# Mixture-of-experts overflow rows in units of 32, in four column groups of TensorE

## The reference

```python
def xattn(query, key):
    a = einsum('bqd,bkd->bqk', query, key)
    return einsum('bqk,bkd->bqd', softmax(a), key)

def ffn(x, W_gate, b_gate, W_e, b_e):
    logits = x @ W_gate + b_gate
    _, top_idx = top_k(logits, 2)
    y_all = relu(einsum('bsd,edh->bseh', x, W_e) + b_e)
    return take_along_axis(y_all, top_idx[..., None], axis=2).mean(axis=2)

x = x + tanh(g_xattn[0]) * xattn(layernorm(x), ctx_4096)
x = x + tanh(g_ffn[0]) * ffn(layernorm(x), W_gate, b_gate, W_e, b_e)
```

## Time and profile before

| | us |
|---|---|
| median of 3 runs | 349.36 |
| lowest, highest | 346.36, 354.34 |
| profiled execution, its own time | 346.13 |
| its span, first to last instruction | 344.2 |

### The profile page before, as it was taken

The page is one execution under the profiler, slowest core; times in us unless marked ns, Lnnn a source line. Parts: engine busy times, 40 slices in busy tenths (PEclk is TensorE's granted clock), DMA queues, the critical chain, the costliest instruction groups (busy, mean ns, idle before and its releaser), DMA issues.

```text
span 344.2 us, 4282 instructions
## 1 busy us (share of the span) xinstructions
PE 316.2 (92%) x1488; PEld 231.1 (67%) x1488; DVE 203.3 (59%) x434; ACT 123.0 (36%) x165; POOL 77.7 (23%) x97
## 2 busy tenths in 40 slices
PE   0989999989999999969999999999999999999960
PEld 0554465555565588748887788888888888888840
DVE  2226368477668886895566885755176675753220
ACT  2223444346435548012544535515031551431000
POOL 6101131110213210402422331530121233111130
PEclk9999999999999999999999999999999999999996
DMA  7999999999989895218999999898469889644142
GB/s 257 309 270 333 348 352 398 392 315 385 375 302 353 303 391 170 70 54 207 398 312 397 368 354 330 237 383 258 63 178 350 269 219 390 189 61 63 18 76 30
DMA packets 24333, 90.57 MB, mean 263 GB/s; under 512 B 2898, under 2 KB 2898, under 8 KB 24302
## 3 DMA queue, kind: packets, MB, share of 16 engines
q1 hardware_dynamic: 13662, 52.86, 42.4%
q0 software_dynamic: 7504, 25.47, 27.6%
q10 hardware_dynamic: 3136, 11.83, 9.9%
HBM read 73.63 MB, written 16.52 MB: 262 GB/s over the span
## 4 chain that ended last, share of the span: by engine, by line
PE 72%; DMA 15%; DVE 6%; issue 2%; ACT 2%; POOL 1%; SPq 0%; DVEq 0%; POOLq 0%
PE ps L442 47%; PE ps L350 9%; PE ps L375 8%; DMA kT<-in_ctx_cols 7%; DMA raw<-in_L_ffn_W_e 4%; PE ps L425 4%; DVE wl L871 3%; DMA xg<-hn_rows,src_token 3%; PE ps L396 2%; PE ps L387 1%; DMA x_all<-in_x 1%; PE ps L341 1%; DVE xl L875 1%; ACT qT L601 1%; DVE stats L728 1%
## 5 line engine op out<-in xcount | busy, mean ns | idle before, releaser
L871 DVE TENSOR_TENSOR wl<-raw,wh 128x1024 fp32r<-128x1024 f32 x64 | 75.7, 1219 | 18.7 <-ACT wh L622 18.6
L442 PE MATMUL ps<-wh,xh 128*128 128x512 f32 x256 | 83.1, 401 | 1.7 <-DVE xl L875 1.7
L442 PE MATMUL ps<-wl,xh 128*128 128x512 f32 x256 | 80.7, 394 | 1.9 <-DVE wl L871 1.9
L442 PE MATMUL ps<-wh,xl 128*128 128x512 f32 x256 | 80.2, 393 | 0.0
L622 ACT ACTIVATE wh<-raw 128x1024 fp32r<-128x1024 f32 x64 | 64.0, 1052 | 29.9 <-DMA raw<-in_L_ffn_W_e 23.0
L442 PEld LDWEIGHTS ps<-wl,xh 128*128 128x128 f32 x256 | 47.8, 188 | 13.4 <-DVE wl L871 2.8
L442 PEld LDWEIGHTS ps<-wh,xl 128*128 128x128 f32 x256 | 48.0, 188 | 10.6
L1054 POOL DMA_INDIRECT out_rows<-y,dst_token x15 | 29.7, 1978 | 109.7 <-DVE y L885 100.3
L442 PEld LDWEIGHTS ps<-wh,xh 128*128 128x128 f32 x256 | 46.3, 189 | 11.3 <-DVE xl L875 2.6
L625 ACT ACTIVATE xh<-ps 128x1024 fp32r<-128x1024 f32 x16 | 16.3, 1020 | 88.8 <-PE ps L425 88.8
L350 PE MATMUL ps<-kT,qT 128*100 128x361 f32 x128 | 44.0, 496 | 1.6 <-ACT qT L601 1.3
(11 more groups left out here) (122 smaller groups left out, 237.5 us busy)
## 6 DMA issues: line engine op xcount, KB each, us to landing
raw<-in_L_ffn_W_e SPq DMA_DIRECT2D x64, 512.0 KB, 9.9
kT<-in_ctx_cols SPq DMA_DIRECT2D x16, 722.0 KB, 16.8
ctx<-in_ctx ACTq DMA_DIRECT2D x8, 1024.0 KB, 13.1
bias<-in_L_ffn_b_e SPq DMA_DIRECT2D x8, 512.0 KB, 12.5
ctx<-in_ctx ACTq DMA_DIRECT2D x8, 420.0 KB, 16.3
out_rows<-x_all POOLq DMA_DIRECT2D x8, 400.0 KB
hn_rows<-hn POOLq DMA_DIRECT2D x8, 400.0 KB
x_all<-in_x SPq DMA_DIRECT2D x7, 400.0 KB
```

The lines of the kernel that those rows point to most:

```text
L442: mm = nc.tensor.matmul(into[:, n * HB:(n + 1) * HB], rows[:, k, :], weights[:, k, n * HB:(n + 1) * HB], start=(k == 0 and c == first), st ...
L871: nc.vector.tensor_tensor(wl[e % 2][:, k, :], raw[e % 2][:, k, :], wh[e % 2][:, k, :], ALU.subtract).then_inc(s_wl, 1)
```

## The change

Rows over the static tiles go in units of 32 rows instead of tiles of 128, up to OVER = 17 units for an expert, so that COLS becomes 8 x 25 = 200. A unit's rows are gathered (32 rows), turned by eight transposes with a 32 x 32 identity, and copied from PSUM by ACT as plain float32 (`x_over`, 128 x 256); neither ACT nor DVE splits them. The product is float32: for each slice k and for each of `wh` and `wl`, four matmuls of 256 columns, the c-th with the c-th quarter of the weights' columns, into PSUM partitions 32c to 32c+31. DVE adds the bias in four instructions on 32 partitions each, and POOL adds 128 quarter rows to the output. The number of units is worked out by the same rule as before, with 32 in the place of 128. In `name_tokens` the static tiles' slots are read in four copies, a quarter of the partitions each, and the units' slots are kept apart and named once, by the new `name_overs`, called between the splits of expert 1's weights, just before `fill_table`.

```diff
+    UNIT = 32
+    GROUPS = P // UNIT
+    HQ = H // GROUPS
+    OVER = -(-HALVES * (HALF_TOK - P) // UNIT)
+    UNITS_E = STATIC_TILES * GROUPS + OVER
+    COLS = E * UNITS_E
...
-        over_rows = sb("over_rows", [P, D])
-        xh_over = sb("xh_over", [P, KD, P], F32R)
-        xl_over = sb("xl_over", [P, KD, P], F32R)
+        over_rows = sb("over_rows", [UNIT, D])
+        x_over = sb("x_over", [P, KD, UNIT])
+        over_y = sb("over_y", [P, HQ])
...
             def turn_over(over_before, j):
-                pe.wait_ge(o_gath, 16 * (over_before + j) + 16)
-                turn_rows(ps[1], over_rows).then_inc(o_xT, 1)
+                wait_apart(pe, o_gath, 16 * (over_before + j) + 16)
+                for k in range(KD):
+                    mm = nc.tensor.transpose(ps[1][:, k * UNIT:(k + 1) * UNIT], over_rows[:, k * P:(k + 1) * P],
+                                             ident[0:UNIT, 0:UNIT])
+                mm.then_inc(o_xT, 1)
...
                 for k in range(KD):
-                    mm = multiply(xh_over, xl_over, e % 2, k, over_ps, (HH, HL, LH), HH, LH)
+                    for w in (wh[e % 2], wl[e % 2]):
+                        for c in range(GROUPS):
+                            mm = nc.tensor.matmul(over_ps[c * UNIT:(c + 1) * UNIT, :], x_over[:, k, :],
+                                                  w[:, k, c * HQ:(c + 1) * HQ].bitcast(F32),
+                                                  start=(k == 0 and w is wh[e % 2]), stop=(k == KD - 1 and w is wl[e % 2]))
...
             def name_tokens(half):
                 dve.wait_ge(s_slots, HALF_B * (half + 1))
-                if half == 0:
-                    link(nc.vector.tensor_copy(acc[:, :], slot_ps))
-                else:
-                    link(nc.vector.tensor_tensor(acc[:, :], acc[:, :], slot_ps, ALU.add))
+                units = slot_ps.rearrange("p (e u) -> p e u", e=E)
+                first = half * (UNITS_E - GROUPS)
+                for c in range(GROUPS):
+                    rows = slice(c * UNIT, (c + 1) * UNIT)
+                    last = nc.vector.tensor_copy(slot_acc[rows, :], units[rows, :, first + c])
+                link(last)
...
+                units = units[:, :, GROUPS:GROUPS + OVER]
                 if half == 0:
+                    nc.vector.tensor_copy(over_acc[:, :, :], units).then_inc(s_over_read, 1)
                 else:
+                    dve.wait_ge(s_over_read, 1)
+                    link(nc.vector.tensor_tensor(over_acc[:, :, :], over_acc[:, :, :], units, ALU.add))
+
+            def name_overs():
+                link(nc.vector.tensor_scalar(over_used[:, :, :], over_acc[:, :, :], 0.0, own_shift[:, 0:1], ALU.is_lt,
                                              ALU.mult))
+                link(nc.vector.scalar_tensor_tensor(out=src_over[:, :, :], in0=over_acc[:, :, :], scalar=own_row[:, 0:1],
+                                                    in1=over_used[:, :, :], op0=ALU.add, op1=ALU.add))
+                link(nc.vector.tensor_scalar(over_used[:, :, :], over_acc[:, :, :], 0.0, spare_shift[0][:, 0:1], ALU.is_lt,
+                                             ALU.mult))
+                link(nc.vector.scalar_tensor_tensor(out=over_used[:, :, :], in0=over_acc[:, :, :],
+                                                    scalar=spare_row[0][:, 0:1], in1=over_used[:, :, :],
+                                                    op0=ALU.add, op1=ALU.add))
+                link(nc.vector.tensor_scalar(dst_over[:, :, :], over_used[:, :, :], float(GROUPS), quarter_no[:, 0:1],
+                                             ALU.mult, ALU.add))
...
                 if k == KD // 2:
+                    name_overs()
                     fill_table()
...
-                    add_rows(over_rows, idx_over[:, 1:2], o_added)
+                    quarters = out.rearrange("n (a d) -> (n a) d", a=GROUPS)
+                    g.indirect_dma_start(quarters, bass.IndirectOffsetOnAxis(idx_over[:, 1:2], 0), over_y[:, :], None,
+                                         compute_op=ALU.add).then_inc(o_added, 16)
```

More of the change, by code:

```diff
@@ L638, in wait_multiplied, with copy_over @@
                     eng.wait_ge(s_wfree, KD * (e + 1))
-            def split_over(over_before, j):
+            def copy_over(over_before, j):
                 act.wait_ge(o_xT, over_before + j + 1)
-                split_rows(xh_over, ps[1]).then_inc(o_xh, 1)
+                nc.scalar.activation(x_over[:, :, :].rearrange("p k m -> p (k m)"), ps[1][:, 0:KD * UNIT], ACT.Copy
+                                     ).then_inc(o_x, 1)
             def load_values(b):
@@ new lines, in name_tokens @@
+                link(nc.vector.scalar_tensor_tensor(out=src_token[:, half, :], in0=slot_acc[:, :], scalar=own_row[:, 0:1],
+                                                    in1=is_used[:, :], op0=ALU.add, op1=ALU.add))
+                link(nc.vector.tensor_scalar(is_used[:, :], slot_acc[:, :], 0.0, spare_shift[half][:, 0:1], ALU.is_lt,
+                                             ALU.mult))
+                nc.vector.scalar_tensor_tensor(out=dst_token[:, half, :], in0=slot_acc[:, :],
+                                               scalar=spare_row[half][:, 0:1], in1=is_used[:, :], op0=ALU.add, op1=ALU.add
+                                               ).then_inc(s_tokens, 1)
@@ L844, in name_tokens @@
[L844 to L847, removed]
-                                             ALU.mult))
@@ L852, in count_first_half @@
             def count_first_half():
                 dve.wait_ge(s_count, 1)
-                link(nc.vector.tensor_scalar(skip[:, :], count_ps, float(P), float(-TILES_E * P), ALU.max, ALU.add))
+                link(nc.vector.tensor_scalar(skip[:, :], count_ps, float(P), float(-UNITS_E * UNIT), ALU.max, ALU.add))
             def fill_table():
@@ L905, in evacuate_over @@
                 dve.wait_ge(o_mm, n + 1)
-                finish(over_ps, e, over_rows, o_yev, n + 2, o_y)
+                for c in range(GROUPS):
+                    rows = slice(c * UNIT, (c + 1) * UNIT)
+                    last = nc.vector.tensor_tensor(over_y[rows, :], over_ps[rows, :],
+                                                   bias[e % 2][rows, c * HQ:(c + 1) * HQ], ALU.add)
+                last.then_inc(o_yev, 1)
+                dve.wait_ge(o_yev, n + 2)
+                nc.vector.tensor_scalar(over_y[:, :], over_y[:, :], 0.0, tgf_half[:, 0:1], ALU.max, ALU.mult
+                                        ).then_inc(o_y, 1)
             norm(0, measure_query(0), 1, 2)
             dve.wait_ge(s_const, 1)
+            link(nc.vector.tensor_scalar(quarter_i[:, :], row_i[:, :], 5, None, ALU.logical_shift_right))
+            link(nc.vector.tensor_copy(quarter_no[:, :], quarter_i[:, :]))
             norm(1, measure_query(1), 1, 2)
@@ L1048, in gather_tile @@
                     pool.wait_ge(s_xT, n - 1)
-                col = column(*ORDER[n])
-                half = ORDER[n][1]
-                gather(xg[n % 2], src_token[:, col:col + 1], s_gath[n % 2], hn_rows[0:HALF_TOK * (half + 1), :])
+                e, half = ORDER[n]
+                gather(xg[n % 2], src_token[:, half, e:e + 1], s_gath[n % 2], hn_rows[0:HALF_TOK * (half + 1), :])
             def add_rows(rows, idx, added):
@@ L1132, in _ @@
             gather_tile(3)
[L1133 removed]
             for part in range(2):
[L1135 removed]
+                g.tensor_scalar(half_row[:, part:part + 1], dst_token[:, HALVES - 1, E - 1:E], 2.0, float(part), ALU.mult, ALU.add
                                 ).then_inc(s_half_row, 1)
```

77 lines of the change are left out of this document (34 added, 43 removed).

## The result

| | before | after |
|---|---|---|
| median | 349.05 us (4 runs) | 367.63 us (4 runs, 365.84 to 370.11) |
| ratio | | 1.0557, 95% interval 1.0497 to 1.0617 |
| profiled execution, its span | 344.2 us | 368.4 us |

What follows compares the result with a forecast made beforehand. PE was taken to bound the kernel, with DVE's naming at 139 to 153 us also on the chain. -4.0 - 0.3 + 0.4 + 0.4 + 1.75 gave about -1.75 us, put on the median 349.36: 347.6 us, range 343.5 to 355.0.

Steps and rivals of the forecast that it cites:

- How many units: Over path: expert 4 has 18 rows over 128, one unit of 32; all others none, so it is taken once.
- The product, -4.0 us: PE's over-tile product: 64 float32 matmuls, four quarters at once, take 7.1 us where it was 11.14.
- Rival 1: PE's unit product: the four quarters run one after another, 27.5 us, kernel 368.0 us; chance 0.16 including fewer than 1.7 at once.
- Rival 2: PE's unit product: quarters run at once but weight loads don't hide, 10.3 us, kernel 350.9; chance 0.14 shared with two at once.
- The 8.7 us: PE's unit product by the Trainium skill's column-group share, 3.2 times for four; whole sum 1.6 us higher.
- rival 4: Over path: several units for expert 4, each another 7 us or more; within the remaining chance of 0.02.
- The turn, -0.3: PE's eight transposes of the unit's rows, within tile 8's products: 0.6 us in place of 0.88.
- The slots, +0.4: PE's slots products: tok_col goes from 56 to 200 columns, 0.065 us more, twice per batch; bounds 0 and 1.1.
- `name_overs`, +1.75: DVE amid expert 1's splits, ahead of fill_table: five linked steps on 136 elements, 1.75 us; bounds 1.3 and 2.2.
- `name_tokens(1)`, +0.4: DVE's naming from the last slots to the first split: 1.75 us where it was 1.39; bounds 0.1 and 0.8.
- The delay at full price: DVE's time added before tile 2 moves the whole stretch behind it and reaches the end in full.
- Rival 3: Stretch behind 153 us set by DMA: DVE's added 2.55 us vanish, only -4.3 is left, kernel 345.1 us; chance 0.06.

Runs made afterwards that it cites:

- e1: Changed kernel without PE's code for an expert's second and further units, which never runs here: 349.39 us, ratio to before 0.9943.
- e5: Kernel before, with the never-run product of an expert's second over tile written five times: 372.04, 374.93, 378.67 and 834.66 us.
- e4: Changed kernel with all four quarters' products sent to output partitions 0 to 31, one column group: 391.53 us in one run.
- e3: Changed kernel with name_overs called twice in a row: 370.67 us, ratio to before 1.0547.
- e10: e7 with name_overs back at the change's place, ahead of fill_table: 349.61 us, ratio to before 1.0031.
- e8: e1 with name_overs moved behind the split of tile 2: 348.43 us, ratio to before 1.0000.
- e9: e7 unchanged, run in more rounds: 347.94 us median of 12 runs, ratio to before 0.9968.
- e2: Kernel before, with the never-run product of an expert's second over tile written twice: 355.63 us, ratio to before 1.0116.
- e7: Changed kernel, PE's unit code written once in a loop, name_overs moved behind the split of tile 2: 344.42, 349.65, 350.60 and 415.99 us.

## Why the prediction was wrong

1. **The step that failed** is "How many units": "All other experts have none, so the new path too is taken once." I counted what the path costs where it is taken, and counted nothing where it is branched over. The stops are 14.3 us in seven pieces, 0.6 of it there before, and with the refilling and tile 13's 1.7 for the half clock about 17 of the 18 us between the medians of the changed kernel and e1. e1 takes it away by deleting code that never runs, e5 brings it into the kernel before by adding such code, and the stops looked at end 1.5 to 2.7 us behind the landing of a piece of code. The forecast had nothing for it, and it is most of the 20 us by which the forecast was too low. The page of before had the hint in the q8 row, 19 pieces of code, and the diff had 64 matmuls twice in each of eight blocks. I priced the matmuls that run and never asked what the others do to the program.
2. **The product, -4.0 us: right.** 7.04 us against 7.1; e4 shows that the column groups do it. Rival 1, quarters in series, is out, although its 368.0 us is what was measured. Rival 2, bare loads, is out too: 10.3 us was its price, so the rule quoted with it doesn't hold here. For column groups that share all rows, loads hide. The 8.7 us set beside the sum were too high as well: four groups gave 3.9 times, not 3.2. There was one unit, 64 products, so rival 4 is out.
3. **The turn, -0.3: right** (0.61 us). **The slots, +0.4: about right** (0.20 us a batch where it was 0.08).
4. **`name_overs`, +1.75: right** (1.76). **`name_tokens(1)`, +0.4: too low**, it was 0.7, within its bounds: the copies of a quarter of the partitions start 0.17 us apart, not 0.07 as my row of two neighbours had it, and the wait ahead of the last add costs 0.2.
5. **The delay at full price: right.** e3 adds 1.8 us for the second call. Rival 3 is out.
6. **Left out as well: the clock.** PE's wait for `wl` grew from 1.6 to 3.9 us, and in all profiles with `name_overs` in that place (changed kernel, e1, e3, e4, e10) the clock is 0.50 at the start of tile 2, which costs 1.8 to 2.6 us (2.1 in the changed kernel). In e8 and e9, with it moved, and in both profiles of before it is 1.00; but in e2, e5 and e7 it fell with waits of 1.5 to 1.9 us too. What decides there stays open. Behind the stops it fell again, in tile 13 for 1.7 us.

With the code short and the naming late, what is left of my sum is about -3 us, and e9's profile shows it from the last `slots` on. So in the profile the change's idea is worth about 1% where it runs once; in whole runs that gain is not shown (0.9919 to 1.0018). Its form cost 5.6%.

## What to carry to other kernels

Price a conditional block at every place where it is branched over too, by the length of its code: unrolled code for rare cases, written once for the first and once more in a loop, can push the branch's target out of what is already fetched, and each such branch stopped the engine for 0.5 to 3.6 us here. Count the instructions in the compiled program, not the calls: a plain float32 matmul has twice as many here as a float32r one. In the profile, look at the packets of the instruction queue next to a stop that nothing explains. And a measured time that meets a rival's number isn't yet that rival: the product was 7 us, not 27.

## What the hardware showed that I had not expected

- An engine without anything to wait for stood 1.3 to 3.6 us at a branch over about 553 instructions, and the trace named a bystander, the evacuation that had just begun, as releaser in five of these cases. PE went on 1.5 to 2.7 us behind the landing of 16 KB of code.
- Four plain float32 matmuls of 32 output rows in four column groups ran in the time of one, 0.43 us a set, with their weight loads hidden: 3.9 times as fast as in one group (27.74 to 7.04 us).
- The same attention stage ended at 139.4 and at 144.9 us in two profiles of the same kernel, which is more than the change's forecast gain.
